# A four-layer Perceiver block on one core: the projections of three cross-attentions as pairs of 64-row products, and the value products of four heads as one series

## The chip, the cores and the metric

The kernel runs on one core of one Trainium2 chip. The metric is the device time of one execution in microseconds. The core's engines are called as in the profile: PE (matrix products; PEld is its weight load), DVE (vector), ACT (scalar), POOL, and SP, which issues DMAs.

## The reference, cut to what matters

Four layers, each a cross-attention, a self-attention and a feed-forward part, work on 128 rows of 256 numbers. The change touches the cross-attentions of layers 0, 2 and 3, where 128 queries attend to 12,544 keys with 16 heads of 16 numbers. That of layer 3 reads:

```
q = split_heads(layernorm(x) @ Wq + bq); k = split_heads(ctx @ Wk + bk); v = split_heads(ctx @ Wv + bv)
logits = q @ k.T / sqrt(16) + mask * -1e9     # layer 0 masks with -inf, layer 2 has no mask
x = x + (softmax(logits) @ v) @ Wo + bo       # layer 0 has no Wo
```

## The kernel before

One function, `cross_attention_turned`, makes these three layers (L0x, L2x, L3x in the names). The keys go in 14 blocks of 896, in seven tiles of 128. A block has 16 **waves**, a wave handles two heads against half a block, and four waves (a **group**) handle four heads (a **quad**): waves 0 and 1 the first four tiles, waves 2 and 3 the last three. For each wave g, PE does:

- `maxima(g, r)`, L915: two products of 448 columns, queries stationary, keys moving, one in array rows 0 to 63 and one in rows 64 to 127 (50 or 52 rows are used). DVE reduces each bank to a maximum (L1151).
- `scores(u)` for wave u = g - LAG, L926: keys stationary, queries moving, 128 columns, in pairs of a low and a high row half. ACT takes the exponential of each bank (L1053) into `prob`, which has three buffers.
- every other wave `values`, L953: 16 or 12 products of 128 rows by 32 columns into `p_oT`, for four heads at once in four column groups. After the last quad, `copy_out` (L1071) copies the bank, `turn_out` (L962) transposes it and `accumulate` (L1184) adds it to `acc`.
- in the other waves one of eight **items** of the next block's projections (`project`). Items 0 to 3 make k (L888: six products of 448 columns), items 4 to 7 make v (L893: six products of 256 columns for each tile; item 7 has one tile, the others two). The six products are three products of split operands (high and low part) for each of two 128-row halves of the 256 inputs. All go to one bank, `p_proj`, which ACT copies out (L1037 k, L1043 v); for k, DVE adds the low part (`k_low`, L1111).
- once a group `turn_q`, L940: two transposes of `nat`, into which DVE has written the quad's maxima (`raise_top` L1165, `split_top` L1175 and L1177). ACT copies them to `q_sub` (L1059).

SP loads the context two blocks ahead and, when a block's k is split, issues 24 DMAs that spread it over `k_stack` (L767); POOL splits the context (L837, L839). The maxima and the scores each go through a ring of three banks: an engine that writes a bank waits until the one that read it three places earlier is done. The order on each engine is fixed by a loop over g, and semaphores count.

Of the kernel before, what the change touches and what calls it, by code (L numbers as in the profile page):

```python
# [635 lines left out]
LAG = 7  # L636
# [8 lines left out]
def cross_attention_turned(nc, st, name, w, mask_kind):  # L645
# [53 lines left out]
    p_proj, p_oT = ps("p_proj"), ps("p_oT")  # L699

    ITEMS = 8
# [3 lines left out]
    LAST_G = WAVE_END + LAG + 5  # L705


    M_BLOCK, M_O = 2 * WAVES + 1, 24
    def m_at(g, i):
        k = g % WAVES  # L710
        return g // WAVES * M_BLOCK + 2 * k + i + (k > 11)
# [4 lines left out]
    S_GROUP, S_Q = 9, 6  # L716
    def s_at(u, i):
        return (u // 4 + 1) * S_GROUP + u % 4 * 2 + i + (u % 4 == 3)
    s_q_at = lambda q: q * S_GROUP + S_Q
    def s_done(n):  # L720
        return 0 if n < S_Q else 1 if n < S_GROUP else n - 7 - (n >= NB * QUADS * S_GROUP + S_Q)


# [3 lines left out]
    v_tiles = lambda i: [t for t in (2 * (i - 4), 2 * (i - 4) + 1) if t < NT]  # L727

    with nc.Block() as block:
# [75 lines left out]
        def _(e):  # L805
# [26 lines left out]
            def split_ctx(b):  # L832
                odd = b % 2
                e.wait_ge(sem("ctx_loaded"), b * 16)
                if b >= 2:
                    e.wait_ge(sem("projected"), (b - 1) * ITEMS)
# [42 lines left out]
        def _(e):  # L879
# [17 lines left out]
            def project_next(b, i):  # L897
                if i == 0:
                    e.wait_ge(sem("ctx_split"), b)
                if i <= 4:  # L900
                    e.wait_ge(sem("k_split"), 4 * b + i)
                if i == 0 or i > 4:
                    e.wait_ge(sem("v_made"), 4 * b + max(i - 4, 0))
                project(b, i, p_proj)
# [14 lines left out]
            def scores(u):  # L919
                b, half = u // WAVES, u % 4 // 2  # L920
                if u % 4 == 0:
                    e.wait_ge(sem("s_free"), s_done(s_q_at(u // 4)))
# [9 lines left out]
            def turn_q(q):  # L932
                n = s_q_at(q)
                e.wait_ge(sem("raised"), 3 * q + 3)
                if n >= S_GROUP:
# [3 lines left out]
                for p in range(2):  # L939
                    mm = e.transpose(s_bank[n % RING][:, p * P:(p + 1) * P], nat[:, 4 * p + q % 4, :], ident[:])  # L940
                mm.then_inc(sem("s_made"), 1)

            def values(k):
                q, half = k // 2, k % 2
                b, j = q // 4, q % 4
                if k % 8 == 0:
                    e.wait_ge(sem("v_made"), (b + 1) * 4)
                    if b:
                        e.wait_ge(sem("oT_copied"), b)
                e.wait_ge(sem("s_free"), s_done(s_at(2 * k + 1, 1)))  # L950
                for at, t in enumerate(tiles_of(half)):
                    for n in range(4):
                        mm = e.matmul(p_oT[32 * n:32 * n + VW, j * P:(j + 1) * P], v[:, b % 2, t, n // 2 * 8 + 2 * j + n % 2, :],  # L953
                                      prob[:, k % 3, n, at, :], start=t == 0, stop=t == NT - 1)
                mm.then_inc(sem("valued"), 1)

            def turn_out(b):
                n = m_o_at(b)
                e.wait_ge(sem("oT_copied"), b + 1)
# [5 lines left out]
            keep_busy(e, p_oT, ident, 4)  # L965
# [4 lines left out]
            keep_busy(e, p_oT, ident, 9)  # L970
            e.wait_ge(sem("k_weights_split"), 1)
            for n, bank in enumerate([p_proj] + m_bank):
                e.wait_ge(sem("ctx_0_split"), 1 + n // 2)
                project(0, FIRST_KEYS[n], bank)
# [16 lines left out]
            project(0, 5, p_oT)  # L991
# [3 lines left out]
            for g in range(LAST_G):  # L995
                u = g - LAG
# [5 lines left out]
                if g == 0:  # L1002
                    project(0, 6, s_bank[0])
                    project(0, 7, p_proj)
# [11 lines left out]
            if has_wo:  # L1016
                e.wait_ge(sem("o_final"), 1)
                for c in range(DC):
                    mm = e.transpose(s_bank[0][:, c * P:(c + 1) * P], o[:, c * P:(c + 1) * P], ident[:])
                mm.then_inc(sem("o2_turned"), 1)  # L1020
                e.wait_ge(sem("o2T_copied"), 1)
                e.wait_ge(sem("out_weights"), 48)
                for c in range(DC):
                    mm = e.matmul(p_proj[:, 0:D], o2T[:, c, :], wo[:, c, :], start=c == 0, stop=c == DC - 1)
# [3 lines left out]
        def _(e):  # L1028

            def evacuate(b, i, bank):  # L1030
                e.wait_ge(sem("projected"), b * ITEMS + (FIRST_KEYS[i] if b == 0 and i < 4 else i) + 1)
# [7 lines left out]
                else:  # L1039
                    tt = v_tiles(i)  # L1040
                    if i == 4 and b >= 2:
                        e.wait_ge(sem("valued"), 8 * (b - 1))
# [4 lines left out]
            def exps(u, r):  # L1047
# [3 lines left out]
                if k >= 3 and u % 2 == 0 and r == 0:  # L1051
                    e.wait_ge(sem("valued"), k - 2)
# [3 lines left out]
            def copy_q(q):  # L1056
                n = s_q_at(q)
                e.wait_ge(sem("s_made"), s_done(n))
                e.copy(q_sub[:, q % 4::4, :], s_bank[n % RING][:, 0:2 * P].rearrange("p (s n) -> p s n", s=2)).then_inc(sem("s_free"), 1)  # L1059
# [6 lines left out]

            def copy_out(b):
                e.wait_ge(sem("valued"), 8 * (b + 1))
                if b:
                    e.wait_ge(sem("m_made"), m_done(m_o_at(b - 1)))  # L1070
                e.copy(oT[:], p_oT[:]).then_inc(sem("oT_copied"), 1)  # L1071
# [10 lines left out]
            for n, bank in enumerate([p_proj] + m_bank):  # L1082
                evacuate(0, FIRST_KEYS[n], bank)
# [5 lines left out]
            for i, bank in enumerate([s_bank[2], p_oT, s_bank[0], p_proj]):  # L1089
                evacuate(0, 4 + i, bank)  # L1090
            for g in range(LAST_G):
                u = g - LAG
# [3 lines left out]
                if u % WAVES == 2 and u > 2:  # L1096
                    copy_out(u // WAVES - 1)
                if g % 2 == 1 and g // WAVES + 1 < NB:
                    evacuate(g // WAVES + 1, g % WAVES // 2, p_proj)
                if g % 4 == 1 and 0 <= g // 4 - 1 < NB * QUADS:  # L1100
                    copy_q(g // 4 - 1)
# [4 lines left out]
        def _(e):  # L1106
# [26 lines left out]
            for n, bank in enumerate([p_proj] + m_bank):  # L1133
                k_low(0, FIRST_KEYS[n], bank)
# [19 lines left out]
            columns = lambda q, n: nat[:, q % 4::4].rearrange("q p (r e) -> q p r e", r=2)[:, :, :, TOP + n]  # L1154

# [31 lines left out]
            for g in range(LAST_G):  # L1187
                u = g - LAG
                if g < WAVE_END:
                    top_of(g, 0)  # L1190

                if g % 2 == 0 and g // WAVES + 1 < NB and 0 < g % WAVES <= 8:
                    k_low(g // WAVES + 1, g % WAVES // 2 - 1, p_proj)
                if g % 4 == 0 and 0 < g <= WAVE_END:
                    raise_top(g // 4 - 1)
                if g < WAVE_END:
                    top_of(g, 1)
                if g % 4 == 0 and 0 < g <= WAVE_END:
                    split_top(g // 4 - 1)
                if u % WAVES == 4 and u > 4:  # L1200
                    accumulate(u // WAVES - 1)
# [13 lines left out]
            if has_wo:  # L1215
# [5 lines left out]
                e.tensor_tensor(x[:], x[:], p_proj[:, 0:D], ALU.add)  # L1221
# [1577 lines left out]
```

## Time and profile before

| | us |
|---|---|
| median of 3 runs | 2401.51 (2388.33 to 2405.67) |
| the profiled execution | 2400.72 |
| its span, first to last instruction | 2398.9 |
| PE busy in the span | 2254.4 |
| DVE busy | 1594.7 |
| ACT busy | 1504.3 |
| mean granted TensorE clock | 0.966 of full speed |

The span leaves out 1.8 us around it. Matmuls are pipelined and their ends modelled, so PE's busy time is no measure of how well it is used.

### The profile page before, as it was taken

Reading aid. Unit: us, or ns where it says so; the run is one execution under the profiler, and the core shown is the slowest. Engines: PE = TensorE matmul, PEld = TensorE weight load, DVE = VectorE, ACT = ScalarE, POOL = GpSimd, SP = SyncE. Lnnn points to the kernel's source line nnn. Section 1 sums busy time; section 2 is a strip of 40 time slices with the busy share of each in tenths; the row PEclk is TensorE's granted clock in tenths of the full one; section 3 lists DMA queues with packets and bytes.
Section 4 is the critical chain, followed back from the end, with each engine's and each line's share of the span. In section 5 each row is a group of like instructions: output and inputs, shape, how many; then the busy total and the mean of one; then the engine's idle time right before and its main releaser. Section 6 shows DMA issues by size and latency. Waiting matters only on the chain. (4 is left out here: it accounts for less than half of the span.)

```text
span 2398.9 us, 68493 instructions
## 1 busy us (share of the span) xinstructions
PE 2254.4 (94%) x26863; PEld 1884.1 (79%) x26863; DVE 1594.7 (66%) x3621; ACT 1504.3 (63%) x3041; POOL 413.5 (17%) x356
## 2 busy tenths in 40 slices
PE   7999999988999999999778999999977999999968
PEld 6888888777788887887756888888866888888758
DVE  6777777635777777777564777777735777777632
ACT  3666666624788787888524666666633666666611
POOL 3222122002221212210002212222003221122000
PEclk9999999989999999999898999999978999999979
DMA  7667776365344354441154766666516667766335
GB/s 148 118 120 121 125 116 122 54 215 155 100 125 113 106 131 102 116 122 41 46 178 98 148 110 116 115 117 116 82 50 141 121 121 126 127 115 119 57 119 190
DMA packets 152460, 279.62 MB, mean 117 GB/s; under 512 B 32829, under 2 KB 72078, under 8 KB 152218
## 3 DMA queue, kind: packets, MB, share of 16 engines
q1 hardware_dynamic: 148842, 272.18, 55.0%
q10 hardware_dynamic: 3376, 4.03, 0.6%
q8 instruction: 175, 2.87, 0.5%
q14 instruction: 67, 0.55, 0.1%
HBM read 120.94 MB, written 0.33 MB: 51 GB/s over the span
## 5 line engine op out<-in xcount | busy, mean ns | idle before, releaser
L1151 DVE TENSOR_REDUCE L3x_tops<-L3x_m_bank 128x1 f32<-128x448 f32 x448 | 262.6, 619 | 124.5 <-PE L3x_m_bank L915 122.4
L1151 DVE TENSOR_REDUCE L0x_tops<-L0x_m_bank 128x1 f32<-128x448 f32 x448 | 262.7, 619 | 121.8 <-PE L0x_m_bank L915 119.6
L1151 DVE TENSOR_REDUCE L2x_tops<-L2x_m_bank 128x1 f32<-128x448 f32 x448 | 262.7, 619 | 118.4 <-PE L2x_m_bank L915 116.3
L559 DVE CUSTOM_DVE_ANT_0 L1x_p_s<-L1x_p_s,L1x_mask,L1x_neg_max 128x512 f32<-128x512 f32 (+1 forms) x400 | 288.7, 742 | 55.7 <-PE L1x_p_s L320 53.1
L452 ACT ACTIVATE L1x_prob<-L1x_p_s,L1x_neg_max 128x512 f32<-128x512 f32 (+1 forms) x400 | 275.0, 687 | 68.2 <-DVE L1x_neg_max L559 66.2
L1053 ACT ACTIVATE L2x_prob<-L2x_s_bank 128x512 f32<-128x512 f32 x448 | 219.6, 542 | 90.9 <-PE L2x_s_bank L926 89.7
L1053 ACT ACTIVATE L0x_prob<-L0x_s_bank 128x512 f32<-128x512 f32 x448 | 219.6, 542 | 89.9 <-PE L0x_s_bank L926 88.7
L1053 ACT ACTIVATE L3x_prob<-L3x_s_bank 128x512 f32<-128x512 f32 x448 | 219.6, 542 | 87.6 <-PE L3x_s_bank L926 86.1
L329 PE MATMUL L1x_p_t<-net_ident,L1x_prob 128*128 128x128 f32 x1568 | 239.4, 274 | 13.8 <-ACT L1x_probT L174 11.4
L329 PEld LDWEIGHTS L1x_p_t<-net_ident,L1x_prob 128*128 128x128 f32 x1568 | 191.8, 140 | 56.9 <-ACT L1x_probT L174 23.6
L320 PE MATMUL L1x_p_s<-L1x_k_stack,L1x_q_stack 96*128 96x512 f32 (+1 forms) x400 | 181.6, 456 | 1.8 <-DVE L1x_q_stack L542 1.8
L174 ACT COPY L1x_probT<-L1x_p_t 128x512 f32<-128x512 f32 (+1 forms) x300 | 172.7, 576 | 1.6 <-PE L1x_p_t L329 1.3
L926 PEld LDWEIGHTS L2x_s_bank<-L2x_q_sub,L2x_k_stack 50*128 50x128 f32 x1568 | 122.8, 189 | 9.6 <-ACT L2x_prob L1053 6.2
L926 PEld LDWEIGHTS L0x_s_bank<-L0x_q_sub,L0x_k_stack 52*128 52x128 f32 x1568 | 122.5, 188 | 9.4 <-ACT L0x_prob L1053 6.3
L926 PEld LDWEIGHTS L3x_s_bank<-L3x_q_sub,L3x_k_stack 52*128 52x128 f32 x1568 | 121.5, 186 | 9.2 <-ACT L3x_prob L1053 6.1
L926 PE MATMUL L2x_s_bank<-L2x_q_sub,L2x_k_stack 50*128 50x128 f32 x1568 | 116.3, 261 | 3.1 <-ACT L2x_prob L1053 2.9
L926 PE MATMUL L0x_s_bank<-L0x_q_sub,L0x_k_stack 52*128 52x128 f32 x1568 | 115.9, 260 | 3.1 <-ACT L0x_prob L1053 2.9
L926 PE MATMUL L3x_s_bank<-L3x_q_sub,L3x_k_stack 52*128 52x128 f32 x1568 | 114.7, 258 | 3.1 <-ACT L3x_prob L1053 2.9
L915 PE MATMUL L3x_m_bank<-L3x_k_stack,L3x_q_max 52*128 52x448 f32 x448 | 109.1, 467 | 7.3 <-DMA L3x_k_stack<-L3x_kT 5.7
L915 PE MATMUL L0x_m_bank<-L0x_k_stack,L0x_q_max 52*128 52x448 f32 x448 | 109.4, 469 | 4.8 <-DMA L0x_k_stack<-L0x_kT 3.2
L915 PE MATMUL L2x_m_bank<-L2x_k_stack,L2x_q_max 50*128 50x448 f32 x448 | 108.7, 466 | 3.3 <-DMA L2x_k_stack<-L2x_kT 1.6
L953 PE MATMUL L2x_p_oT<-L2x_prob,L2x_v 128*32 128x128 f32 x3136 | 111.6, 281 | 0.0
(766 smaller groups left out, 4464.0 us busy)
## 6 DMA issues: line engine op xcount, KB each, us to landing
L0x_k_stack<-L0x_kT SPq DMA_DIRECT2D x333, 112.0 KB, 4.1
L2x_k_stack<-L2x_kT SPq DMA_DIRECT2D x333, 112.0 KB, 4.0
L3x_k_stack<-L3x_kT SPq DMA_DIRECT2D x333, 112.0 KB, 4.0
L1x_k_stack<-L1x_kT SPq DMA_DIRECT2D x288, 128.0 KB, 2.4
L3f_w<-in_L_ffn_w SPq DMA_DIRECT2D x16, 1024.0 KB, 8.2
L0f_w<-in_L_ffn_w SPq DMA_DIRECT2D x48, 256.0 KB, 5.1
L1x_ctx<-in_ctxT SPq DMA_DIRECT2D x24, 512.0 KB, 3.9
L0x_ctx<-in_ctxT SPq DMA_DIRECT2D x13, 896.0 KB, 6.7
```

The lines of the kernel that those rows point to most:

```text
L174: copy(probT[:, h % PT_RING, 0:nk], p_t[h % T_RING][:, 0:nk]).then_inc(sem(copied(h)), 1)
L320: e.matmul(p_s[h % S_RING][:, 0:nk], q_stack[0:ROWS, h, :], k_stack[0:ROWS, odd, h // 2, 0:nk], start=True, stop=True).then_inc(sem("score ...
L329: i = e.transpose(p_t[h % T_RING][:, t * P:(t + 1) * P], prob[:, h % P_RING, t * P:(t + 1) * P], ident[:])
L452: e.activation(prob[:, h % P_RING, 0:nk], p_s[h % S_RING][:, 0:nk], ACT.Exp, bias=neg_max[:, odd, h:h + 1], scale=-1.0).then_inc(sem("expe ...
L559: e.tensor_tensor_reduce(s, s, mask[:, odd, 0:nk], -1.0, neg_max[:, 1 - odd, h:h + 1], ALU.add, ALU.min, neg_max[:, odd, h:h + 1]).then_in ...
L915: e.matmul(m_bank[n % RING][:, 0:HALF], q_max[rows_of(r), slot_of(g), :], k_stack[rows_of(r), b % 2, slot_of(g), half * HALF:(half + 1) * ...
L926: mm = e.matmul(s_bank[s_at(u, r) % RING][:, at * P:(at + 1) * P], k_stack[rows_of(r), b % 2, slot_of(u), t * P:(t + 1) * P], q_sub[rows_o ...
L953: mm = e.matmul(p_oT[32 * n:32 * n + VW, j * P:(j + 1) * P], v[:, b % 2, t, n // 2 * 8 + 2 * j + n % 2, :], prob[:, k % 3, n, at, :], star ...
L1053: e.activation(prob[:, k % 3, u % 2 * 2 + r, 0:nt, :].rearrange("p t n -> p (t n)"), s_bank[n % RING][:, 0:nt * P], ACT.Exp).then_inc(sem( ...
L1151: e.tensor_reduce(tops[:, b % 2, h, half:half + 1], m_bank[n % RING][:, 0:HALF], AX, ALU.max).then_inc(sem("m_free"), 1)
```

## The change

Only `cross_attention_turned` changes; LAG becomes 8.

- **Projections.** `p_oT` is gone and its bank becomes `p_proj[1]`. Two items are a pair and are made together: each 128-row product becomes two products of 64 rows, and a product in the low half of the array for one bank alternates with one in the high half for the other bank. In turn 0 bank 0 takes the low rows and bank 1 the high rows, in turn 1 the other way round. Each turn is cut into a third and two thirds, which stand in waves 2, 3 (ahead of the scores), 3 (behind them) and 0. A group thus makes one pair.
- **Seventh value tile.** In the last pair (items 6 and 7) it is a partial sum over the low rows in bank 0 and over the high rows in bank 1; DVE copies the one and adds the other (`last_values`).
- **Values.** The 28 products of a quad are one series, in wave 1, right behind the two transposes and into the same bank of the scores' ring (columns 256 to 383). ACT copies both out in wave 2. `prob` and `v` are guarded by that order, and the waits on `valued` go.
- **Split of the maxima.** `split_top` now stands ahead of the wave's second reduction on DVE.
- **Tail.** Behind each of the last eight waves of scores, and ahead of the last transposes and the output product, PE does `keep_busy` products with the identity into `p_proj[1]`, which nobody reads.

```diff
-LAG = 7
+LAG = 8
...
-    p_proj, p_oT = ps("p_proj"), ps("p_oT")
+    p_proj = [ps(f"p_proj{i}") for i in range(2)]
...
+            def pair_products(b, i, r, bank):
+                odd, rows = b % 2, half_rows(r)
+                item = 2 * i + bank
+                out = p_proj[bank]
+                terms = [(wp, cp, c) for wp, cp in PRODUCTS for c in range(DC)]
+                if i < 2:
+                    keys = slice(bank * HALF, (bank + 1) * HALF)
+                    return [(out[:, 0:HALF], wk_part[rows, wp, c, i * P:(i + 1) * P], ctx_part[rows, odd, cp, c, keys])
+                            for wp, cp, c in terms]
+                tiles = v_tiles(item) if i == 2 else (4 + bank, NT - 1) if r == bank else (4 + bank,)
...
+            def project_round(b, i, turn, third):
+                x, y = pair_products(b, i, turn, 0), pair_products(b, i, 1 - turn, 1)
...
+                for k in range(first, last):
+                    if turn and k == 0:
+                        e.wait_ge(sem("half_x_made"), pair_count(b, i))
+                    mm = e.matmul(*x[k], start=turn == 0 and k == 0, stop=turn == 1 and k == len(x) - 1)
...
+                    if k < len(y):
...
+                        mm = e.matmul(*y[k], start=turn == 0 and k == 0, stop=turn == 1 and k == len(y) - 1)
...
+            def values(q, bank):
...
+                for t in range(NT):
+                    for n in range(4):
+                        mm = e.matmul(bank[32 * n:32 * n + VW, 2 * P:3 * P], v[:, b % 2, t, n // 2 * 8 + 2 * j + n % 2, :],
+                                      prob[:, (2 * q + t // 4) % 3, n, t % 4, :], start=t == 0, stop=t == NT - 1)
+                return mm
+
+            def turns_and_values(group):
...
+                if q is not None:
+                    mm = turn_q(q, s_bank[n % RING])
+                if group % 4 == 2 and group >= 6:
+                    turn_out(group // 4 - 1)
+                if old is not None:
+                    mm = values(old, s_bank[n % RING])
                 mm.then_inc(sem("s_made"), 1)
...
+                if wave == 3 and pair:
+                    project_round(*pair, 0, 1)
                 if 0 <= u < WAVE_END:
                     scores(u)
-                if u % 2 == 1 and 0 <= (u - 3) // 2 < NB * 8:
-                    values((u - 3) // 2)
-                if u % WAVES == 4 and u > 4:
-                    turn_out(u // WAVES - 1)
-                if g % 2 == 1 and g // WAVES + 1 < NB:
-                    project_next(g // WAVES + 1, g % WAVES // 2)
-                if g % 4 == 1 and 0 <= g // 4 - 1 < NB * QUADS:
-                    turn_q(g // 4 - 1)
+                    if g >= WAVE_END:
+                        keep_busy(e, p_proj[1], ident, 3)
+                if wave == 1 and (turned_at(group - 1) is not None or valued_at(group - 1) is not None):
+                    turns_and_values(group - 1)
...
+                if wave == 2 and pair:
+                    project_round(*pair, 0, 0)
+                if wave == 3 and pair:
+                    project_round(*pair, 1, 0)
+                if wave == 0 and pair:
+                    project_round(*pair, 1, 1)
...
+            def last_values(b):
...
+                e.tensor_copy(out, high).then_inc(sem("v_last_half"), 1)
+                e.wait_ge(sem("v_last_half"), b)
+                e.tensor_tensor(out, out, low, ALU.add).then_inc(sem("v_last_made"), 1)
```

## Rows read from the trace of the kernel before

**Rows 1.** The page: busy time of the engines.

```profile
PE 2254.4 (94%) x26863; PEld 1884.1 (79%) x26863; DVE 1594.7 (66%) x3621; ACT 1504.3 (63%) x3041; POOL 413.5 (17%) x356
```

**Rows 2.** Table of stretches: L2x from block 1 on, and its tail.

```profile
1334.00:1741.70 407.70, 405.73 (x5723) 340.19 (x5722) 297.16 (x631) 279.93 (x590) 76.35 (x61) 1.00 0.66 111
1741.70:1766.30 24.60, 18.09 (x211) 13.28 (x206) 4.44 (x13) 8.79 (x20) 0.88 (x2) 0.60 0.01 1
```

**Rows 3.** Waits of PE's weight loads, 1364 to 1731 us: total, times, longest.

```profile
PEld L2x_m_bank L915 <- issue: 28.0, 136, 0.3
PEld L2x_m_bank L915 <- DVE L2x_tops L1151: 5.8, 28, 0.4
```

**Rows 4.** Timeline of PE, L2x, a group with two k items, and one block later.

```profile
1399.36 0.48 PE L915 MATMUL L2x_m_bank<-L2x_k_stack,L2x_q_max 50*128 50x448 f32 x2
1399.67 0.56 PE L926 MATMUL L2x_s_bank<-L2x_q_sub,L2x_k_stack 50*128 50x128 f32 x8
1400.17 0.86 PE L953 MATMUL L2x_p_oT<-L2x_prob,L2x_v 128*32 128x128 f32 x24
1400.96 0.47 PE L915 MATMUL L2x_m_bank<-L2x_k_stack,L2x_q_max 50*128 50x448 f32 x2
1401.27 0.44 PE L926 MATMUL L2x_s_bank<-L2x_q_sub,L2x_k_stack 50*128 50x128 f32 x6
1401.64 1.48 PE L888 MATMUL L2x_p_proj<-L2x_ctx_part,L2x_wk_part 128*128 128x448 f32 x6
1402.96 0.38 PE L940 MATMUL L2x_s_bank<-net_ident,L2x_nat 128*128 128x128 f32 x2
1403.27 0.47 PE L915 MATMUL L2x_m_bank<-L2x_k_stack,L2x_q_max 50*128 50x448 f32 x2
...
1403.96 1.08 PE L953 MATMUL L2x_p_oT<-L2x_prob,L2x_v 128*32 128x128 f32 x32
1404.97 0.47 PE L915 MATMUL L2x_m_bank<-L2x_k_stack,L2x_q_max 50*128 50x448 f32 x2
1405.28 0.56 PE L926 MATMUL L2x_s_bank<-L2x_q_sub,L2x_k_stack 50*128 50x128 f32 x8
1405.76 1.51 PE L888 MATMUL L2x_p_proj<-L2x_ctx_part,L2x_wk_part 128*128 128x448 f32 x6
1407.20 0.47 PE L915 MATMUL L2x_m_bank<-L2x_k_stack,L2x_q_max 50*128 50x448 f32 x2
...
1431.18 0.47 PE L915 MATMUL L2x_m_bank<-L2x_k_stack,L2x_q_max 50*128 50x448 f32 x2
```

**Rows 5.** Timeline of PE, L2x, v items of twelve and of six products.

```profile
1645.00 0.66 PE L962 MATMUL L2x_m_bank<-net_ident,L2x_oT 128*128 128x128 f32 x4
1645.41 1.67 PE L893 MATMUL L2x_p_proj<-L2x_wv_part,L2x_ctx_part 128*128 128x256 f32 x12
1647.02 0.47 PE L915 MATMUL L2x_m_bank<-L2x_k_stack,L2x_q_max 50*128 50x448 f32 x2
...
1653.62 0.98 PE L893 MATMUL L2x_p_proj<-L2x_wv_part,L2x_ctx_part 128*128 128x256 f32 x6
1654.53 0.48 PE L915 MATMUL L2x_m_bank<-L2x_k_stack,L2x_q_max 50*128 50x448 f32 x2
```

**Rows 6.** Timeline behind the last maxima of L2x, where scores wait for exponentials.

```profile
1742.24 1.16 DVE L1151 TENSOR_REDUCE L2x_tops<-L2x_m_bank 128x1 f32<-128x448 f32 x2 [0.98 <-PE L2x_m_bank L915]
1742.64 1.09 ACT L1053 ACTIVATE L2x_prob<-L2x_s_bank 128x512 f32<-128x512 f32 x2 [0.93 <-PE L2x_s_bank L926]
1743.29 0.66 PE L926 MATMUL L2x_s_bank<-L2x_q_sub,L2x_k_stack 50*128 50x128 f32 x8 [0.68 <-ACT L2x_prob L1053]
```

**Rows 7.** Timeline of SP's queue, L2x: issues of one block's stack.

```profile
1385.02 14.96 SPq L767 DMA_DIRECT2D L2x_k_stack<-L2x_kT  x17
```

**Rows 8.** The page, DMA issues: count, KB each, median us to landing.

```profile
L2x_k_stack<-L2x_kT SPq DMA_DIRECT2D x333, 112.0 KB, 4.0
```

**Rows 9.** The split of the maxima: ns least/median/most, first and last start.

```profile
L1175 DVE CAST L2x_nat<-L2x_top x55: 157/164/2895, 1313.9 to 1738.3; 128x4 fp32r<-128x4 f32 x55
```

More of the change, by code:

```diff
@@ L895, in project @@
                 mm.then_inc(sem("projected"), 1)
[L897 to L904, printed above, removed]
+            def pair_products(b, i, r, bank):
[8 more added lines that the diff above has]
+                tiles = v_tiles(item) if i == 2 else (4 + bank, NT - 1) if r == bank else (4 + bank,)
+                return [(out[:, n * D:(n + 1) * D], ctx_part[rows, odd, cp, c, t * P:(t + 1) * P], wv_part[rows, wp, c, :])
+                        for n, t in enumerate(tiles) for wp, cp, c in terms]
@@ L921, in scores @@
                 if u % 4 == 0:
-                    e.wait_ge(sem("s_free"), s_done(s_q_at(u // 4)))
+                    e.wait_ge(sem("q_copied"), u // 4 + 1)
+                if u % 4 == 3 and turned_at(u // 4 + 1) is not None:
+                    e.wait_ge(sem("q_copied"), u // 4 + 2)
                 e.wait_ge(sem("s_free"), s_done(s_at(u, 1) - RING))
@@ L938, in turn_q @@
                     e.wait_ge(sem("v_made"), 4)
-                for p in range(2):
-                    mm = e.transpose(s_bank[n % RING][:, p * P:(p + 1) * P], nat[:, 4 * p + q % 4, :], ident[:])
-                mm.then_inc(sem("s_made"), 1)
[L943 to L955, printed above, removed]
+                if q is not None:
[4 more added lines that the diff above has]
+                    mm = values(old, s_bank[n % RING])
+                mm.then_inc(sem("s_made"), 1)
             def turn_out(b):
                 n = m_o_at(b)
-                e.wait_ge(sem("oT_copied"), b + 1)
+                e.wait_ge(sem("s_free"), s_done(s_q_at(4 * b + 3 + 2)))
                 e.wait_ge(sem("m_free"), m_done(n - RING))
@@ L995, in _ @@
             for g in range(LAST_G):
-                u = g - LAG
+                u, group, wave = g - LAG, g // 4, g % 4
+                pair = pair_at(group - 1 if wave == 0 else group)
                 if g < WAVE_END:
@@ L1020, in _ @@
                 mm.then_inc(sem("o2_turned"), 1)
+                keep_busy(e, p_proj[1], ident, 3)
                 e.wait_ge(sem("o2T_copied"), 1)
@@ L1088, in _ @@
                             kT[of:of + HD, 0, part].bitcast(F32)).then_inc(sem("k_stacked_0_0"), 16)
-            for i, bank in enumerate([s_bank[2], p_oT, s_bank[0], p_proj]):
+            for i, bank in enumerate([s_bank[2], p_proj[1], s_bank[0], p_proj[0]]):
                 evacuate(0, 4 + i, bank)
             for g in range(LAST_G):
-                u = g - LAG
+                u, group, wave = g - LAG, g // 4, g % 4
+                pair = pair_at(group - 1)
+                if wave == 1 and pair:
+                    evacuate(pair[0], 2 * pair[1], p_proj[0])
+                    evacuate(pair[0], 2 * pair[1] + 1, p_proj[1])
+                if wave == 2 and (turned_at(group - 1) is not None or valued_at(group - 1) is not None):
+                    copy_turned_and_valued(group - 1)
                 if 0 <= u < WAVE_END:
@@ L1132, in _ @@
             e.wait_ge(sem("k_bias"), 16)
-            for n, bank in enumerate([p_proj] + m_bank):
+            for n, bank in enumerate([p_proj[0]] + m_bank):
                 k_low(0, FIRST_KEYS[n], bank)
@@ L1154, in _ @@
             columns = lambda q, n: nat[:, q % 4::4].rearrange("q p (r e) -> q p r e", r=2)[:, :, :, TOP + n]
+            def last_values(b):
+                e.wait_ge(sem("pair_x_made"), pair_count(b, 3))
+                e.wait_ge(sem("pair_y_made"), pair_count(b, 3))
+                e.wait_ge(sem("v_made"), 4 * b + 4)
+                high, low = (p_proj[n][:, D:2 * D].rearrange("p (h d) -> p h d", h=HX) for n in range(2))
+                out = v[:, b % 2, NT - 1, :, 0:HD]
+                e.tensor_copy(out, high).then_inc(sem("v_last_half"), 1)
+                e.wait_ge(sem("v_last_half"), b)
+                e.tensor_tensor(out, out, low, ALU.add).then_inc(sem("v_last_made"), 1)
             def raise_top(q):
```

141 lines of the change are left out of this document (94 added, 47 removed).

## The prediction

> **What bounds the kernel now.** I read the page's busy times first: PE 2254 us of 2398.9, DVE 1595, ACT 1504 [rows 1]. PE's figure is modelled, so I asked for a steady stretch of L2x: 407.7 us with PE busy 405.7, DVE 297, ACT 280, and the clock at 1.00, its upper level of 2.4 GHz [rows 2]. Then the waits of PE's weight loads over 367 us: 28.0 us in 136 waits for nothing the profile shows, 5.8 for DVE, no ACT or DMA row worth naming [rows 3]. So PE's own order sets the pace, and other engines only have to keep up. L0x and L3x run the same waves. The timeline shows the pace: the same wave comes back after 31.8 us, one block [rows 4].
>
> In that timeline the distance from one kind of work to the next matters, not the busy time. The maxima take 0.31 us until the scores start, though one product of 448 columns streams in 0.187 us at 2.4 GHz (448 / 2.4) and two serial ones would need 0.37: **the two row halves run at once**, and some 0.12 us is exposed in front [rows 4]. Eight score products take 0.48, six 0.37: 0.11 for a pair of 128-column products [rows 4]. Value series of 24 and 32 records take 0.79 and 1.01, so 0.22 a tile and 0.13 on top [rows 4]. A k item takes 1.44 (6 x 0.20 + 0.23), v items of 12 and 6 products 1.61 and 0.91 (0.117 each, 0.21 on top), transposes 0.31 for two and 0.41 for four [rows 4, 5].
>
> The part "on top" is what is paid each time the array goes from one shape to another: the first product of the new shape starts some 0.2 us after the last of the old. It appears at every change between row halves (maxima, scores), full rows (projections, transposes) and column groups (values), and hardly between maxima and scores, which share a shape. The Trainium skill, TensorEngine Tiling (Array Packing), section Key Properties, says that changing the tiling mode "drains the TensorE"; the rows agree, with about 0.2 us a time.
>
> **The change part by part.** All sums are for one block with projections.
>
> *Before*, by the same pieces: a group with two k items is 4 x 0.31 maxima, 0.50 + 0.37 + 0.38 + 0.48 scores, 0.79 + 1.01 values, 1.32 + 1.44 items and 0.31 transposes, 7.84 us; the rows give 1407.20 - 1399.36 = 7.84 [rows 4].
>
> *64-row projections.* They stream as many columns as before: 12 pairs of 448 in a k group, 24 and 18 pairs of 256 in the two v groups. No row shows two accumulating 64-row products. From below, a pair costs what one full-row product costs now, 0.20 and 0.12 [rows 4, 5], if the halves overlap as they do in the maxima; from above each half waits for the other, 0.19 and 0.11 more a pair. The maxima are nearest in size and have the same two halves and two banks, so I take 0.20 and 0.12. They now stand beside maxima and scores of the same shape: those change no shape, and the 0.12 in front of the maxima goes in three waves of four (0.20 instead of 0.31). Doubled weight loads hide beside the streams: scores already do two loads and two products in 0.11.
>
> *One value series.* 7 x 0.22 + 0.13 = 1.67 instead of 1.80. It stands behind the two transposes (0.31, taken whole, though transposes and values differ in shape; between no change of shape and one, 0 to 0.2, I take the 0.1 that 0.31 holds beyond 2 x 0.11). So only one round trip a group leaves the row halves.
>
> *Sum of a group:* maxima 0.31 + 3 x 0.20 = 0.91; scores 4 x 0.11 + 4 x 0.11 + 3 x 0.11 + 3 x 0.11 + 0.04 = 1.58; transposes and values 1.98. That is 4.47, and with projections 6.87 (k, 12 x 0.20), 7.35 (24 x 0.12) and 6.63 (18 x 0.12); the last one also has turn_out, 0.41. A block: 2 x 6.87 + 7.35 + 7.04 = 28.1 us.
>
> *New waits.* The scores' ring is the tight one: scores of wave u need the first exponential of wave u-1. Two exponentials of 512 columns take 1.09 and start right behind the scores; the next scores start 0.65 after them [rows 6]. From the last score pair that is 0.86 us for four tiles and, with a shorter exponential, 0.74 for three, and 0.16 to the first new product. Between waves 3 and 0 stand only a third of a turn and the maxima: k gives a stall of 0.2 us, the v groups 0.1 and 0.35. In the last pair the cut between waves 0 and 1 (8 of 24 products, 0.48 us) adds 0.2. Together 2 x 0.2 + 0.1 + 0.35 + 0.2 = 1.1 us. In wave 1 ACT has two copies of k and two exponentials, some 2.2 us, beside 2.0 us of transposes and values: hidden. Behind a stalled score on PE wait its round and the next maxima, so DVE too.
>
> *DVE.* 32 reductions at about 0.55 (two take 1.16 [rows 6]), four k_low at under 0.7, maxima and splits at 0.6 a group, plus 0.8 for `last_values`: some 24 us of 29; hidden on average. The transposes follow the split by about 0.7 us where they had nearly 2 before, and the split's first copy is sometimes 0.6 to 2.9 us long instead of 0.16 [rows 9]. I add 0.3 us a block for that and for sporadic waits. The earlier split delays only a reduction.
>
> *DMA.* SP issues a block's 24 copies in about 0.85 us each (17 in 14.96) and they land 4.0 later [rows 7, 8]. The first quad's six are due at the next block; they land about 9 us after k is split, near 18 us of 29.5: hidden with 2 us to spare, where it was 5.
>
> *Block:* 28.1 + 1.1 + 0.3 = 29.5 instead of 31.8, **2.3 us less**. Twelve blocks a layer have their projections and a full set of other work: 3 x 12 x 2.3 = 83 us.
>
> *Ends.* The first block is filled with maxima and projections, where DVE is as busy as PE; I take 2.5 us a layer gained. The last block has no projections and waits on the exponentials before and after: 1.2 us lost. The tail (24.6 us in L2x at a mean granted clock of 0.60, so mostly at the lower level, 1.2 GHz [rows 2]) gets a wave more and products nobody reads: at the low level these cost, at the high one they repay themselves. I take 1 us lost, from -3 to +3. Together 3 x (-2.5 + 1.2 + 1.0), about -1 us.
>
> **Sum:** 2400.7 - 83 - 1 = 2317 us for an execution like the profiled one, 0.8 us below the median: 2316 us.
>
> **The rivals.**
>
> *Overlap fails (slower).* The accumulating halves share something that the maxima don't. Serial, a block pays 24 x 0.187 + 42 x 0.107 = 9.0 us: 39 x 9.0 = 351, so 2667 us. The gain of 84 us is 2.15 a block, so it decides from 2.15 / 66 pairs = 0.03 us a pair on. For it: nothing in the trace accumulates in both halves. Against: maxima and scores overlap fully, and the values accumulate four at once. A partial loss of 0.3 of the stream is 2.7 us a block, 2316 + 105 = 2421 us. The Trainium skill speaks for this one: TensorE: Matmul & The Clock Gate, section Measured speedup vs the span model, has a speedup of 3.07 for four row tiles, not 4, which as an estimate is 0.3 more a stream. In this trace maxima show no such loss. Chance 8% for both.
>
> *The waits move to the rings.* ACT and DVE are each over 80% busy in a group and the banks are three. If queues behind the copies of wave 1 and late splits cost 1.1 us a block more, 39 x 1.1 = 43: 2360 us. For it: the 0.2 to 0.35 us stalls above leave no play. Against: wave 1 gives both engines 2 us to catch up. Chance 23%.
>
> *The stack comes late.* If k's split slips by 3 us, the next block waits for its DMAs: 1.5 us more a block, 2375 us. Chance 4%.
>
> *It gains the whole switch.* Most stalls vanish behind play elsewhere: 28.3 a block, 39 x 1.2 = 47 less than forecast, 2269 us. Chance 12%.
>
> *The forecast,* 2316 us, 53%. That the change doesn't do what it says would show as a block still at 31.8: inside the rivals above.
>
> **How the numbers follow.** 1% of the time, 24 us, is about what a measurement can tell from no change. Forecast, gain and rings cases and the late stack are faster by over 1%, less where the rings cost twice as much: 84% faster, 8% same (half of the partial loss, the worst of the rings), 8% slower. The range runs from the full gain, 2270, to the late stack, 2375; it leaves out the failed overlap and the far side of the outer cases, under 2 in 10.
>
> **What the profile should show.** L2x's blocks 29.5 us apart; maxima to scores 0.20 in waves 3, 0 and 1 and 0.31 only in wave 2, behind the values; k pairs 0.20 and v pairs 0.12 apart with both halves starting within some ns; 56 value records in one series of 1.6 to 1.7 us; PE waits for ACT's exponentials in waves 0, about 0.2 us each; SP's stack as before. The prediction is wrong if pairs start alternately at double distance, if DVE's reductions become back to back in all waves, or if the transposes wait for the split in most blocks.

## The result and the profile after

The changed kernel takes 2372.7 us (median of 11 runs, 2359.64 to 2393.96) against 2403.59 (11 runs, 2388.33 to 2406.73): a ratio of 0.9888, 95% interval 0.9866 to 0.9909. It is 1.1% faster where 3.5% was forecast, and 2372.7 lies just inside the range. The profiled execution took 2370.45 us; its span is 2368.6, 30.3 less than before. The page's busy times, against [rows 1]:

```profile
PE 2218.0 (94%) x29659; PEld 1905.6 (80%) x29659; DVE 1624.9 (69%) x3699; ACT 1476.5 (62%) x3173; POOL 414.3 (17%) x356
```

They tell little: PE's is 36 us less, though nothing was taken out of its work. Where the time went shows when each layer is cut at the starts of its maxima (L915 before, L961 after). Sums over L0x, L2x and L3x of the two profiled executions, in us:

| stretch of the three layers | before | after | difference |
|---|---|---|---|
| block 0 | 97.6 | 90.2 | -7.4 |
| blocks 1 to 12 | 1150.5 | 1086.3 | -64.2 |
| block 13 (no projections) | 70.9 | 94.7 | +23.8 |
| from the last maxima to the layer's end | 62.3 | 74.1 | +11.8 |

The rest of the 30.3 is 5.7 us more ahead of the first maxima and in parts that the change doesn't touch; single executions of those differ by about a microsecond each (L1x took 592.3 and 593.4).

**So 72 us were gained and 36 given back at the ends of the layers.** The table of stretches of the changed kernel shows where; L2x, steady blocks, block 13, tail; behind the busy times stand the granted clock, the DMA share and GB/s:

```profile
1350.00:1685.00 335.00, 332.03 (x5688) 293.48 (x5684) 266.44 (x570) 235.29 (x545) 68.98 (x55) 1.00 0.72 122
...
1686.00:1716.00 30.00, 29.01 (x338) 22.48 (x331) 15.74 (x37) 14.46 (x34) 0.67 (x1) 0.66 0.25 37
1716.00:1743.80 27.80, 27.04 (x330) 23.10 (x330) 4.80 (x14) 10.74 (x25) 0.89 (x2) 0.87 0.01 2
```

and the same view of the kernel before, block 13 of L2x:

```profile
1718.00:1742.40 24.40, 24.02 (x382) 18.18 (x380) 18.53 (x45) 16.82 (x38) 1.03 (x3) 1.00 0.33 47
```

Block 13 had the full clock before (1.00, 2.4 GHz) and has a mean of 0.66 over these 30 us now, so it stands mostly at 1.2 GHz. Over the whole block the granted clock is 0.77, 0.69 and 0.78 in L0x, L2x and L3x. It falls 7.7 to 9.2 us into the block; until then PE has gone through its groups of maxima, scores and values in L2x without a gap of more than 0.18 us by the trace's modelled ends. The tail is another matter: its clock is 1.00, 0.88 and 1.00 in the three layers, and was 0.69, 0.60 and 0.92 before. It got longer although its clock got higher. The timeline of PE in block 13:

```profile
1699.21 1.11 PE L974 MATMUL L2x_s_bank<-L2x_q_sub,L2x_k_stack 50*128 50x128 f32 x8 [0.18 <-ACT L2x_prob L1117]
1700.26 0.69 PE L983 MATMUL L2x_s_bank<-net_ident,L2x_nat 128*128 128x128 f32 x2
1700.87 3.22 PE L994 MATMUL L2x_s_bank<-L2x_prob,L2x_v 128*32 128x128 f32 x56
1704.02 0.74 PE L961 MATMUL L2x_m_bank<-L2x_k_stack,L2x_q_max 50*128 50x448 f32 x2
```

The value series takes 3.22 us. In a steady block the same series (28 products, which the trace shows as 56 records) takes 1.74. PE's timeline there, the counterpart of [rows 4]:

```profile
1383.00 0.39 PE L961 MATMUL L2x_m_bank<-L2x_k_stack,L2x_q_max 50*128 50x448 f32 x2
1383.33 0.66 PE L974 MATMUL L2x_s_bank<-L2x_q_sub,L2x_k_stack 50*128 50x128 f32 x8
1383.92 0.44 PE L983 MATMUL L2x_s_bank<-net_ident,L2x_nat 128*128 128x128 f32 x2
1384.29 1.74 PE L994 MATMUL L2x_s_bank<-L2x_prob,L2x_v 128*32 128x128 f32 x56
1385.95 0.47 PE L961 MATMUL L2x_m_bank<-L2x_k_stack,L2x_q_max 50*128 50x448 f32 x2
1386.27 0.44 PE L974 MATMUL L2x_s_bank<-L2x_q_sub,L2x_k_stack 50*128 50x128 f32 x6
...
1387.01 0.36 PE L942 MATMUL L2x_p_proj<-L2x_ctx_part,L2x_wk_part 64*128 64x448 f32 x1
1387.01 0.36 PE L948 MATMUL L2x_p_proj<-L2x_ctx_part,L2x_wk_part 64*128 64x448 f32 x1
1387.20 0.36 PE L942 MATMUL L2x_p_proj<-L2x_ctx_part,L2x_wk_part 64*128 64x448 f32 x1
...
1387.40 0.37 PE L961 MATMUL L2x_m_bank<-L2x_k_stack,L2x_q_max 50*128 50x448 f32 x2
1387.62 0.37 PE L942 MATMUL L2x_p_proj<-L2x_ctx_part,L2x_wk_part 64*128 64x448 f32 x1
...
1388.78 0.38 PE L961 MATMUL L2x_m_bank<-L2x_k_stack,L2x_q_max 50*128 50x448 f32 x2
1389.15 0.66 PE L974 MATMUL L2x_s_bank<-L2x_q_sub,L2x_k_stack 50*128 50x128 f32 x8
```

The two halves of a pair (L942, L948) start together and the next pair 0.19 to 0.21 later; pairs of 256 columns are 0.12 apart (1401.53, 1401.65, 1401.77). Two accumulating halves cost what one full-row product did. Behind the values the maxima still take 0.32 until the scores (1385.95 to 1386.27), beside products of their own shape 0.22 (1387.40 to 1387.62). And in wave 0 the scores start 0.37 behind the maxima (1388.78 to 1389.15) where 0.2 would do: they wait. The waits of PE's weight loads, 1350 to 1700 us, against [rows 3]:

```profile
PEld L2x_s_bank L974 <- issue: 15.1, 47, 0.4
PEld L2x_m_bank L961 <- issue: 9.3, 46, 0.4
...
PEld L2x_s_bank L974 <- ACT L2x_prob L1117: 3.6, 14, 0.5
```

The idle time has moved from the maxima to the scores (L974), which had no issue row before, and for ACT 1.1 us in four waits. (The stretch reaches 17 us into block 13; up to 1682 us the three rows read 14.4, 8.7 and 2.4.) An undisturbed steady block takes 29.98 us; with sporadic waits the mean over blocks 2 to 12 is 30.1 to 30.3.

### The profile page after: what moved, and what is told of

Read it like the earlier page. It is cut to its first block and busy times, and to the rows that moved or that the text cites. A ratio compares the mean times of both kernels' runs of the same rounds, so it can differ in the third digit from the quotient of the medians.

```text
span 2368.6 us, 74094 instructions
## 1 busy us (share of the span) xinstructions
PE 2218.0 (94%) x29659; PEld 1905.6 (80%) x29659; DVE 1624.9 (69%) x3699; ACT 1476.5 (62%) x3173; POOL 414.3 (17%) x356
## 5 line engine op out<-in xcount | busy, mean ns | idle before, releaser
L974 PEld LDWEIGHTS L2x_s_bank<-L2x_q_sub,L2x_k_stack 50*128 50x128 f32 x1568 | 120.3, 191 | 26.9 <-issue 19.0
L974 PEld LDWEIGHTS L0x_s_bank<-L0x_q_sub,L0x_k_stack 52*128 52x128 f32 x1568 | 119.0, 189 | 26.4 <-issue 18.5
L974 PEld LDWEIGHTS L3x_s_bank<-L3x_q_sub,L3x_k_stack 52*128 52x128 f32 x1568 | 118.0, 188 | 26.3 <-issue 18.4
L974 PE MATMUL L2x_s_bank<-L2x_q_sub,L2x_k_stack 50*128 50x128 f32 x1568 | 125.1, 271 | 4.3 <-ACT L2x_prob L1117 4.2
L974 PE MATMUL L0x_s_bank<-L0x_q_sub,L0x_k_stack 52*128 52x128 f32 x1568 | 124.0, 269 | 4.2 <-ACT L0x_prob L1117 4.2
L974 PE MATMUL L3x_s_bank<-L3x_q_sub,L3x_k_stack 52*128 52x128 f32 x1568 | 123.0, 267 | 4.3 <-ACT L3x_prob L1117 4.1
L345 PE MATMUL L1x_p_oT<-L1x_probT,L1x_v 128*32 128x128 f32 x3136 | 106.4, 276 | 0.5 <-ACT L1x_probT L174 0.5
L994 PE MATMUL L2x_s_bank<-L2x_prob,L2x_v 128*32 128x128 f32 x3136 | 102.9, 285 | 0.1
L961 PE MATMUL L3x_m_bank<-L3x_k_stack,L3x_q_max 52*128 52x448 f32 x448 | 97.2, 400 | 5.3 <-DMA L3x_k_stack<-L3x_kT 4.2
L961 PE MATMUL L0x_m_bank<-L0x_k_stack,L0x_q_max 52*128 52x448 f32 x448 | 98.2, 404 | 4.2 <-DMA L0x_k_stack<-L0x_kT 3.2
```

What stands on the lines that cost most here:

```text
L345: i = e.matmul(p_oT[VW * s:VW * s + VW, g * P:(g + 1) * P], v[:, odd, t, h, :], probT[:, h % PT_RING, t * P:(t + 1) * P], start=t == 0, st ...
L961: e.matmul(m_bank[n % RING][:, 0:HALF], q_max[rows_of(r), slot_of(g), :], k_stack[rows_of(r), b % 2, slot_of(g), half * HALF:(half + 1) * ...
L994: mm = e.matmul(bank[32 * n:32 * n + VW, 2 * P:3 * P], v[:, b % 2, t, n // 2 * 8 + 2 * j + n % 2, :], prob[:, (2 * q + t // 4) % 3, n, t % ...
```

## The experiments

In all of them but the one with full rows, the granted clock of L2x's steady blocks is 1.00. Each ratio is to the kernel before as it was timed beside that experiment: 2404.06 us for the filler in block 13, the tail without added products, the full rows and the whole tile; 2397.86 for the one pair, the filler without the tail's products, the tail's filler of the same shape and the half cut; 2398.11 for the last two. So ratios compare better than medians. Block and tail times are those of one profiled execution each.

"Steady blocks" are blocks 1 to 12, and "block 13" and "tail" are the last two stretches of the table above, for L0x, L2x and L3x in this order. In the changed kernel they are 30.3, 33.4, 31.1 and 21.7, 27.8, 24.6 us; before they were 23.6 in each layer and 19.3, 24.0, 19.0.

**Filler in block 13.**

```diff
+            def filler(n):
+                e.wait_ge(sem("v_made"), NB * 4)
+                e.wait_ge(sem("v_last_made"), NB - 1)
+                for _ in range(n):
+                    for r in range(2):
+                        e.matmul(p_proj[r][:, 0:HALF], wk_part[half_rows(r), HIGH, 0, 0:P],
+                                 ctx_part[half_rows(r), 0, HIGH, 0, 0:HALF], start=True, stop=True)
...
                 if wave == 0 and pair:
                     project_round(*pair, 1, 1)
+                if WAVE_END - WAVES + 2 <= g < WAVE_END and wave != 1:
+                    filler(3)
```

> Adds, in the last block of each of the three layers (which has no projections), three pairs of 64-row products of 448 columns behind the scores of waves 2, 3 and 0, into the two projection banks; nobody reads them. Clock theory: in the changed kernel the last block takes 30.3, 33.4 and 31.1 us against 23.6 before because PE, without projections and with its values in one lump, is granted the lower clock (0.69 in the stretch, value series of 3.22 us instead of 1.67). The filler, 9 x 3 x 0.20 us minus what stands in idle time, holds the clock at 1.00: last block 25 to 27 us, the run 15 to 25 us shorter than the changed kernel. Ring theory: the last block is long because scores wait for exponentials; the filler only adds: last block 32 us or more, run 0 to 10 us longer.

Measured: 2353.36 us, ratio to before 0.9788 (0.9735 to 0.984). The filler stands in eleven waves, where the expectation counts nine, so it is 33 pairs a layer. Block 13 takes 25.85 us in each layer, at the clock's upper level. Table of stretches of this run, block 13 and tail of L2x, then its timeline:

```profile
1682.00:1709.00 27.00, 27.00 (x448) 23.71 (x446) 16.67 (x39) 17.64 (x41) 0.89 (x2) 1.00 0.17 28
...
1701.50:1725.60 24.10, 23.92 (x338) 20.76 (x334) 4.51 (x13) 10.27 (x25) 0.88 (x2) 1.00 0.01 2
```

```profile
1691.66 1.74 PE L1002 MATMUL L2x_s_bank<-L2x_prob,L2x_v 128*32 128x128 f32 x56
1693.32 0.47 PE L969 MATMUL L2x_m_bank<-L2x_k_stack,L2x_q_max 50*128 50x448 f32 x2
```

More work made the block shorter by 4.4 to 7.5 us. The clock was the cause and the wait for exponentials was not: those fit into 25.85 us. The other experiments bear this out. In all six kernels with three pairs, block 13 takes 25.7 to 26.0 us in each layer, at 1.00. In the four kernels that leave it as the changed kernel has it, the same code takes 27.8 us at a granted clock of 0.88 (twice, with full-row projections ahead of it), 30.3 to 31.1 at 0.77 or 0.78, 31.9 to 32.6 at 0.73 or 0.74, and 33.4 to 33.9 at 0.65 to 0.69. That is 0.35 us for each microsecond at the lower level, and drawn on to 1.00 some 25.4 us, an estimate from these twelve stretches. So how much block 13 loses differs from execution to execution; that it loses does not.

The tails of L0x, L2x and L3x are 21.1, 23.9 and 23.9.

**One pair instead of three.** The same edit with `filler(1)`.

> As the first experiment, with one pair instead of three in each place of the last block. If the little that it adds to PE's work is enough for the clock, the last block is 24.5 to 26 us at a granted clock of 1.00. If it is too little, the clock falls in some of the layers and their last blocks take 28 us or more, value series 3.2 us.

Measured: 2358.08 us, 0.9828 (0.9776 to 0.9879). Block 13: 25.4, 27.0, 25.4. In L2x one series is slow, and only in part:

```profile
1712.28 2.38 PE L1002 MATMUL L2x_s_bank<-L2x_prob,L2x_v 128*32 128x128 f32 x56
```

So in this execution 0.2 us more of products in three waves of four kept the clock at 1.00 in two layers; in the third, L2x, it fell once (0.94 over the block). One execution doesn't show how safe that is.

**No added products in the tail.** The four `keep_busy` calls that the change adds are gone.

> The changed kernel without the added products with the identity in the tail of each layer. Theory one (they cost more than they give): the tail from the last maxima on, 21.7, 27.8 and 24.6 us in the changed kernel, falls by 2 to 3 us a layer, the run by 6 to 9 us. Theory two (they hold the clock): without them the granted clock of the tail falls from about 0.88 to 0.6, value series take 3.2 us instead of 1.67, and each tail grows by 3 to 5 us, the run by 9 to 15.

Measured: 2376.96 us, 0.9899 (0.9866 to 0.9932), not to be told from the changed kernel. Tails 24.0, 28.8 and 28.4 us; in the stretch of L2x the clock is 0.62 instead of 0.87:

```profile
1718.00:1747.00 29.00, 21.45 (x250) 16.15 (x248) 5.05 (x14) 10.66 (x25) 0.88 (x2) 0.62 0.00 1
```

The products do lift the clock, as the second theory says (0.72, 0.62 and 0.67 without them, 1.00, 0.88 and 1.00 with them), and these tails differ by 2.3, 1.0 and 3.8 us. Single executions carry only a part of that: with full rows and with the whole tile, further down, the tail is the changed kernel's, products and all, and takes 24.9, 27.8, 24.6 and 24.9, 24.6, 24.6. So L3x's 3.8 us stands clear, L2x's is 1.0 to 4.2, and L0x's 2.3 is not shown. In both kernels the clock falls in block 13, but when the tail begins it is back at the upper level, or comes back within 0.2 us; in L2x it falls again some 3.5 us later. The expectation of the next experiment has it that the clock had fallen before the tail, and leaves that out.

**Filler in block 13, none in the tail.** Both edits.

> The filler of the first experiment in the last block, and none of the added products with the identity in the tail. Taken alone, leaving those out made each tail longer (24.0, 28.8, 28.4 us against 21.7, 27.8, 24.6), but there the clock had fallen before the tail began. If they hold the clock, the tails here grow from 21.1, 23.9, 23.9 us to 24 to 27 and the run by 4 to 9 us; if a clock that is high at the start of the tail is enough, the tails shrink by 1 to 2 us each.

Measured: 2347.81 us, 0.9804 (0.9742 to 0.9865). Tails 21.4, 24.4 and 24.3: 0.3 to 0.4 us longer than with the products, neither what the one nor what the other theory said. The clock of L2x's tail is between:

```profile
1699.60:1724.00 24.40, 17.44 (x252) 13.54 (x249) 4.43 (x13) 10.19 (x25) 0.89 (x2) 0.83 0.00 1
```

A tail that loses the upper level late (in L2x 9 us behind its start) costs nearly as much as one that holds it with products that take time themselves.

**Filler of the same shape in the tail.** To the first experiment:

```diff
                     if g >= WAVE_END:
-                        keep_busy(e, p_proj[1], ident, 3)
+                        filler(3)
```

> The filler of the first experiment, and in the tail three pairs of 64-row products (0.6 us) behind each wave of scores in place of three products with the identity (0.65 us and two changes of array shape). Shape theory: each of eight score waves gets about 0.3 us shorter in the tail, until the exponentials bound it; tails of 24 us go to 22, run 4 to 6 us shorter than the first experiment's 2353. Rival (exponentials bound the tail already): tails within 0.5 us of 24.

Measured: 2346.28 us, 0.9789 (0.9739 to 0.9838). Tails 20.0, 22.9 and 22.9, each 1.0 us shorter than in the first experiment, at the full clock:

```profile
1699.70:1722.60 22.90, 22.51 (x336) 18.09 (x333) 4.39 (x13) 10.16 (x24) 0.90 (x2) 1.00 0.01 1
```

Half of what the shape theory wanted (2 us), beyond what the rival allowed (0.5): two changes of shape a wave cost, but the exponentials soon bound it. In the total, 1 us a layer can't be seen.

**Full-row projections in the same places.**

```diff
-                    return [(out[:, 0:HALF], wk_part[rows, wp, c, i * P:(i + 1) * P], ctx_part[rows, odd, cp, c, keys])
+                    return [(out[:, 0:HALF], wk_part[:, wp, c, i * P:(i + 1) * P], ctx_part[:, odd, cp, c, keys])
...
-                x, y = pair_products(b, i, turn, 0), pair_products(b, i, 1 - turn, 1)
+                x = item_products(b, i, turn)
...
-                tiles = v_tiles(item) if i == 2 else (4 + bank, NT - 1) if r == bank else (4 + bank,)
+                tiles = v_tiles(item) if i == 2 else (4, NT - 1) if bank == 0 else (5,)
```

> The projections stand in the same places of the order and stream the same columns, but as 128-row products, one bank in turn 0 and the other in turn 1; the seventh value tile is whole, in bank 0, and DVE only copies it. Switch theory: eight more changes of array shape a group, each 0.15 to 0.2 us, so a steady block of L2x goes from 30.0 to 35 to 36.5 us and the run to 2560 to 2620. Rival (the gain came from the single value series and the order, not from the shape): block 30 to 31.8 us, run below 2440.

Measured: 2598.03 us, 1.0836 (1.0734 to 1.0939). L2x's blocks 1 to 12 take 35.6 us on average instead of 30.1, 5.5 us for 32 more changes of shape: 0.17 each. That average holds more than the changes: wave 9 takes 4.1 us instead of 2.8, and the clock is 0.99. An undisturbed block is 34.3 us against 30.0, 0.13 each, in which waits of the changed kernel may be filled. PE's timeline around a wave 3:

```profile
1502.69 0.47 PE L953 MATMUL L2x_m_bank<-L2x_k_stack,L2x_q_max 50*128 50x448 f32 x2
1503.10 0.74 PE L940 MATMUL L2x_p_proj<-L2x_wv_part,L2x_ctx_part 128*128 128x256 f32 x4
1503.77 0.55 PE L966 MATMUL L2x_s_bank<-L2x_q_sub,L2x_k_stack 50*128 50x128 f32 x6
1504.25 0.74 PE L940 MATMUL L2x_p_proj<-L2x_wv_part,L2x_ctx_part 128*128 128x256 f32 x4
1504.91 0.47 PE L953 MATMUL L2x_m_bank<-L2x_k_stack,L2x_q_max 50*128 50x448 f32 x2
```

Four products of 0.12 take 0.67 and 0.66 to the next kind of work, so 0.19 is the price of one change there. The order of the changed kernel is a loss of 194 us without its 64-row form; the form pays for it. The values are one series here too, so that part alone explains nothing of the gain in this order.

**The seventh tile whole, in bank 0.**

```diff
-                tiles = v_tiles(item) if i == 2 else (4 + bank, NT - 1) if r == bank else (4 + bank,)
+                tiles = v_tiles(item) if i == 2 else (4, NT - 1) if bank == 0 else (5,)
...
-                e.tensor_copy(out, high).then_inc(sem("v_last_half"), 1)
-                e.wait_ge(sem("v_last_half"), b)
-                e.tensor_tensor(out, out, low, ALU.add).then_inc(sem("v_last_made"), 1)
+                e.tensor_copy(v[:, b % 2, NT - 1, :, 0:HD], whole).then_inc(sem("v_last_made"), 1)
```

> 64-row pairs as in the changed kernel, but the seventh value tile is made whole in bank 0, so that bank 1 has only six products a turn beside twelve and the last six of a turn have no partner; DVE copies the tile instead of copying one half and adding the other. If PE sets the pace, six more unpaired steps of 0.12 us in each of two turns: block 30.0 to 30.7 us, run 28 us longer. If the added vector work or the stalls behind it cost as much, the run changes by less than 8 us.

Measured: 2383.2 us, 0.9918 (0.9884 to 0.9953); the intervals of this and of the changed kernel overlap. Blocks 1 to 12 average 30.4, 30.5 and 30.5 us against 30.2, 30.1 and 30.2. Of the 0.7 us about 0.2 to 0.5 arrives, between the two theories: wave 0 behind that pair, which waited for an exponential, becomes 0.17 shorter (1.37 instead of 1.54 from maxima to maxima), so the longer pair fills part of a wait. And a product without a partner need not be alone: one (L942) starts together with one of the next maxima (L961), presumably that of the other half (the trace doesn't name the half):

```profile
1449.15 0.28 PE L942 MATMUL L2x_p_proj<-L2x_wv_part,L2x_ctx_part 64*128 64x256 f32 x1
1449.15 0.36 PE L961 MATMUL L2x_m_bank<-L2x_k_stack,L2x_q_max 50*128 50x448 f32 x1
1449.27 0.28 PE L942 MATMUL L2x_p_proj<-L2x_wv_part,L2x_ctx_part 64*128 64x256 f32 x1
1449.39 0.36 PE L961 MATMUL L2x_m_bank<-L2x_k_stack,L2x_q_max 50*128 50x448 f32 x1
```

An undisturbed block is 30.3 us against 30.0, so the two partial sums are worth about 0.3 us a block. (The expectation counts six more steps in each of two turns; there are six more in all, which is the 0.7 us it names.)

**Turn 1 cut in half.** To the first experiment:

```diff
-                    first, last = (0, len(x) // 3) if third == 0 else (len(x) // 3, len(x))
+                    first, last = (0, len(x) // 2) if third == 0 else (len(x) // 2, len(x))
```

> The filler of the first experiment, and turn 1 of each pair cut in half instead of one third and two thirds, so that more products stand between the scores of wave 3 and those of wave 0. Ring theory (scores of wave 0 wait 0.2 us for the exponential in k groups, 0.1 in the first v group): 0.25 to 0.4 us less a steady block, L2x from 29.98 to 29.6 to 29.7, run 8 to 14 us shorter than the first experiment. Rival (the wait moves to the next wave whole): block within 0.1 us of 29.98.

Measured: 2348.27 us, 0.9788 (0.9728 to 0.9847). An undisturbed steady block goes from 29.98 to 29.51 us, 0.47 less: the ring theory, by a bit more than it asked. From maxima to maxima, the waves 0, 1, 2, 3 of the four groups of an undisturbed block of L2x (us):

```
changed kernel   1.54 2.95 1.45 1.37 | 1.70 2.76 1.44 1.37 | 1.70 2.76 1.60 1.49 | 1.79 3.19 1.60 1.26
cut in half      1.30 3.07 1.45 1.58 | 1.29 2.81 1.45 1.58 | 1.29 2.81 1.60 1.73 | 1.37 3.19 1.59 1.37
```

In the k groups wave 3 takes 0.2 more products and wave 0 loses 0.2 of products and 0.2 of waiting. The total shows nothing of it: the ratio is 0.9788 in both, and the 5 us between the medians is also between the two timings of the kernel before. In the profiled execution sporadic waits, in wave 9 above all (mean 3.0 to 3.15 us instead of 2.81), add up to 20 us over the 36 steady blocks, 10 in the first experiment; that they come from the cut is not shown.

**All three together:** filler in block 13, half cut, same-shape filler in the tail.

> Filler in the last block, turn 1 cut in half, and the tail's filler in the row halves' own shape, together. If the three are independent: last block 25.8 us, steady block 29.5, tails 20, 22.9 and 22.9 us, run 2338 to 2345, ratio to before 0.975 or below.

Measured: 2338.2 us (2326.17 to 2350.06), 0.9759 (0.973 to 0.9787). Block 13 25.8, 25.7, 25.8; steady block 29.52; tails 20.0, 22.9, 22.9. The stretches are as expected and add up; the ratio is 0.976 where 0.975 or below was expected. This is 1.3 points better than the changed kernel.

**POOL's long subtraction in seven pieces.**

```diff
-                e.tensor_tensor(ctx_part[:, odd, LOW], ctx[:], ctx_part[:, odd, HIGH].bitcast(F32),
-                                ALU.subtract).then_inc(sem("ctx_split"), 1)
+                for n in range(7):
+                    keys = slice(n * P, (n + 1) * P)
+                    low = e.tensor_tensor(ctx_part[:, odd, LOW, :, keys], ctx[:, :, keys], ctx_part[:, odd, HIGH, :, keys].bitcast(F32),
+                                          ALU.subtract)
+                low.then_inc(sem("ctx_split"), 1)
```

> As the three together, with POOL's subtraction that makes the low part of the context in seven pieces of one key tile instead of one instruction of 4.0 us. If DVE's small copy in the split of the maxima is long (up to 2.9 us instead of 0.16) because POOL's long instruction holds it off, its longest falls to 1 us or less and wave 9 of the steady blocks, 2.9 to 3.1 us on average in the runs so far, comes near its undisturbed 2.81: 4 to 10 us less in the run. Rival (it waits for something else): durations and wave 9 as before.

Measured: 2332.74 us, 0.973 (0.9707 to 0.9753), not to be told from the last. The small copy's longest in L0x, L2x and L3x goes from 3.47, 1.47, 2.85 to 1.52, 1.69, 1.27 us, so it falls in two layers of three and in none to 1 us or less; its rows in L3x, least, median and most in ns, in the kernel with all three

```profile
L1263 DVE CAST L3x_nat<-L3x_top x56: 171/172/2852, 1786.9 to 2197.6; 128x4 fp32r<-128x4 f32 x56
```

and with the pieces:

```profile
L1266 DVE CAST L3x_nat<-L3x_top x56: 171/172/1270, 1793.4 to 2200.1; 128x4 fp32r<-128x4 f32 x56
```

But wave 9 is 2.90, 3.10 and 2.99 us on average against 2.81, 2.89 and 3.02: no gain, and wave 13, which takes 3.18 undisturbed, is 3.43, 3.39 and 3.38 against 3.20, 3.18 and 3.49. That POOL's instruction holds the copy off is neither shown nor refuted: one execution each, and longest values alone. What makes the waits sporadic stays open.

## Why the prediction was wrong

The profiled execution gained 30.3 us where 84 were forecast. Of the 54 missing, 29 are in block 13 and the tail, 19 in the steady blocks, and 5.7 outside the stretches that the forecast prices.

- **The step that failed is "Ends", first for block 13.** "The last block has no projections and waits on the exponentials before and after: 1.2 us lost". Measured, block 13 loses 23.8 / 3 = 7.9 us a layer. I counted it at the full clock since it had 1.00 before, and asked only how long its chain of waits was; no rival held that the clock could fall. The same maxima, scores and value products in another order, with values in one lump and three waves of maxima and scores alone, were granted 0.69 to 0.78. At 1.00 the block takes 25.4 us with one pair of filler (L0x, L3x), 1.8 above before, filler included. So the waits were too small by at most 0.6 us, and the other 6 us a layer are the clock.
- **"Ends", the tail.** "I take 1 us lost" against 11.8 / 3 = 3.9, outside the stated -3 to +3. Here the step that failed is not the clock, which was higher than before (1.00, 0.88, 1.00 against 0.69, 0.60, 0.92), but the price of the added wave and products. Of the 11.8 us, 5.2 went with filler in block 13 (3.9 of them in L2x, whose tail was granted 0.88), 3.1 with products in the array's own shape, and 3.6, or 1.2 a layer, stayed at 1.00. In L3x the best tail is 22.9 us where the kernel before took 19.0 at 0.92. From the last maxima on there are now nine waves of scores instead of eight, and the values stand in three whole series of 1.67 us, during which ACT has sat idle for 1.5 to 1.9 us each (L3x); how the rest divides between them was not tried.
- **The first block: luck.** 7.4 us gained in the three layers, 7.5 forecast. But block 0 stands partly at the lower level, for another time in each execution: 29.0 to 31.4 us in the changed kernel, 28.9 to 36.9 in those with the same code there, where it was 30.3 to 35.0 before. In L2x, where it varies least, 1.3 us are gained where 2.5 were forecast. Two single executions don't show the term right.
- **A steady block: mechanism right, gain too large.** 64.2 us measured, 83 forecast. The overlap of the halves, which no row had shown, is complete, so the failed overlap is refuted: pairs at 0.20 and 0.12. The 0.2 us for a change of shape comes out in the other direction in the full-row experiment, at 0.13 to 0.19. The sum of 28.1 + 1.1 without sporadic waits is 29.2, the block 29.98. Of the 0.8 missing, waves 1 hold 0.41 (the two transposes take 0.37 to the values, not 0.31, and scores to transposes 0.51 to 0.59, not 0.48), waves 0 hold 0.28 (the wait for the exponential is longer than I took it), waves 2 and 3 0.11.
- **Sporadic waits** average 0.1 to 0.3 us a block, as put down. Before, they came to 0.05 to 0.2.
- **The rings** were the right place and not the rival's size: cutting turn 1 in half wins 0.47 us a block. DVE's reductions never became the bound, and the stack of k never came late.
- **The tail's products**, "at the low level these cost, at the high one they repay themselves": the first half no run shows. With block 13 at the full clock they give 0.3 to 0.4 us, in the array's current shape 1.0 more.
- **A slip in the sum.** The profiled execution was 0.8 us below the median, so 2317 for one like it is 2318 for the median and not 2316. It decides nothing.
- **Luck in the range.** 2372.7 lies inside 2270 to 2375, but the upper bound was set for a stack of k that comes late, and the stack was never late.

## What to carry to other kernels

Where a change takes work out of gaps or puts it in lumps, price every stretch again by its clock, above all those where some of the work is missing: here the last of 14 blocks gave back over a third of what twelve had won. Cheap products of the shape that the array has already, in waves with nothing else to do, won it back at once, and three pairs were safer than one. Count changes of array shape on the timeline, at 0.13 to 0.19 us each here, before counting products. Two 64-row halves into two banks ran as one, also when they accumulate: 0.20 us for 448 columns, 0.12 for 256. And read several executions of a stretch before trusting its time: block 0 took anything from 28.9 to 36.9 us in kernels that share its code.

## What the runs showed of the hardware that was not expected

- A stretch with the same kinds of products kept the clock at 1.00 in one order (23.6 us for block 13 of L2x) and got 0.69 in another (33.4 us), though no gap between products there is longer than 0.18 us; 0.2 us of extra products in three waves of four brought two of three layers back to 25.4 us. Which property of the order decides was not tried.
- Two accumulating 64-row products of 448 columns start within 0.03 us of each other and repeat every 0.19 to 0.21 us; serial they would need 0.37. Products without a partner ran beside maxima and scores: one started at the same 1449.15 us as one of the maxima.
- Added work can shorten a kernel: 33 pairs of products that nobody reads, in each of three layers, took 19 us off the median.
